# Two graph-attention layers: scores on eight array tiles, shared PSUM banks, two operations moved to GpSimd

## The reference

```
x = layernorm(x + L0(x, adj))     # q, k, v with biases; scores / sqrt(32) + beta * adj,
                                  # -9e15 where adj is 0; softmax over keys; times v
x = layernorm(x + L1(x, adj))     # q, k without bias, v with bias; scores * 384^-0.5 + adj;
                                  # rows that are all 0 give 0; softmax; times v; @ Wo.T + bo
```

## Time and profile before

| | |
|---|---|
| median of three runs | 1083.22 us (1083.09 to 1083.26) |
| the profiled execution's own time | 1081.61 us |
| its span, first to last instruction | 1079.7 us, TensorE clock granted 0.996 |
| PE, weight loads | 1051.8 us busy (97%), 914.4 (85%) |
| DVE | 935.1 (87%) |
| ACT | 445.9 (41%) |
| POOL | 533.0 (49%) |
| POOL shift (L785), scale (L791), rstd (L806) | 1664, 1474, 547 ns each, 128 times |
| DVE normalise (L657) | 486 to 526 ns, 128 times |
| DVE low part of activations (L669), first and second layer | 1607 and 550 ns |

### The profile page before, as it was taken

The page is one execution under the profiler, slowest core; times in us unless marked ns, Lnnn a source line. Parts: engine busy times, 40 slices in busy tenths (PEclk is TensorE's granted clock), DMA queues, the critical chain, the costliest instruction groups (busy, mean ns, idle before and its releaser), DMA issues.

```text
span 1079.7 us, 38267 instructions
## 1 busy us (share of the span) xinstructions
PE 1051.8 (97%) x16896; PEld 914.4 (85%) x16896; DVE 935.1 (87%) x1642; ACT 445.9 (41%) x713; POOL 533.0 (49%) x454
## 2 busy tenths in 40 slices
PE   7999999999999999999999999999999999999975
PEld 5887888888888888888888888888888888888874
DVE  4799998989899898998989899898998989878786
ACT  4454434444334443444444344443444444344321
POOL 0454554545446454454545546455454544655443
PEclk9999999999999999999999999999999999999998
DMA  7321112112021111111111121120211210010101
GB/s 243 100 70 28 55 46 66 31 51 60 17 66 39 43 61 39 44 46 43 54 43 41 44 66 39 43 61 25 58 39 43 60 44 10 17 36 2 34 31 38
DMA packets 61749, 53.32 MB, mean 49 GB/s; under 512 B 35984, under 2 KB 55440, under 8 KB 61584
## 3 DMA queue, kind: packets, MB, share of 16 engines
q1 hardware_dynamic: 60752, 49.69, 15.4%
q10 hardware_dynamic: 832, 1.18, 0.3%
HBM read 38.28 MB, written 12.58 MB: 47 GB/s over the span
## 4 chain that ended last, share of the span: by engine, by line
PE 92%; DVE 4%; issue 2%; DMA 1%; ACT 1%; POOL 1%; SPq 0%; POOLq 0%; DVEq 0%
PE ps_u L356 54%; PE ps_s L373 10%; PE ps_o L356 9%; PE ps_p L441 7%; PE ps_p L456 7%; PE ps_x L386 3%; PE ps_o L470 2%; DMA xt_in<-in_x_t 1%; DVE row_sum L693 1%; DVE probs L641 1%; POOL probs L785 1%; DVE row_max L651 1%; ACT probs L563 0%; DVE x L657 0%; DVE xt_lo L669 0%
## 5 line engine op out<-in xcount | busy, mean ns | idle before, releaser
L785 POOL TENSOR_TENSOR probs<-probs,row_max 128x768 f32<-128x768 f32 x128 | 213.0, 1664 | 298.1 <-DVE row_max L651 298.1
L791 POOL TENSOR_TENSOR probs<-probs,row_inv 128x768 f32<-128x768 f32 x128 | 188.7, 1474 | 111.1 <-DVE row_inv L701 63.5
L532 ACT COPY probs_t<-ps_p 128x768 f32<-128x768 f32 x128 | 102.7, 802 | 201.7 <-PE ps_p L441 201.7
L563 ACT ACTIVATE probs<-probs 128x768 f32<-128x768 f32 x128 | 108.5, 847 | 78.8 <-POOL probs L785 78.7
L693 DVE TENSOR_REDUCE row_sum<-probs 128x12 f32<-128x768 f32 x128 | 121.5, 949 | 22.5 <-ACT probs L563 21.6
L356 PE MATMUL ps_u<-w_hi_v,xt_lo 128*128 128x384 f32 x384 | 137.3, 358 | 1.0 <-DVE v_sb L686 1.0
L806 POOL TENSOR_TENSOR rstd<-var_eps,minus_half 128x1 f32<-128x1 f32 x128 | 70.0, 547 | 133.8 <-DVE var_eps L734 133.8
L356 PE MATMUL ps_u<-w_hi_v,xt_hi 128*128 128x384 f32 x384 | 129.1, 336 | 0.0
L356 PE MATMUL ps_u<-w_lo_v,xt_hi 128*128 128x384 f32 x384 | 128.7, 335 | 0.0
L651 DVE TENSOR_REDUCE row_max<-probs 128x12 f32<-128x768 f32 x128 | 121.3, 948 | 2.2
L356 PE MATMUL ps_u<-xt_hi,w_lo_q 128*128 128x512 f32 x285 | 121.8, 427 | 0.0
(11 more groups left out here) (78 smaller groups left out, 2034.3 us busy)
## 6 DMA issues: line engine op xcount, KB each, us to landing
x_in<-in_x SPq DMA_DIRECT2D x16, 768.0 KB, 4.6
out<-z SPq DMA_DIRECT2D x64, 192.0 KB, 1.9
xt_in<-in_x_t SPq DMA_DIRECT2D x15, 768.0 KB, 4.5
adj<-in_adj SPq DMA_DIRECT2D x64, 128.0 KB, 2.9
xt_in<-in_x_t SPq DMA_DIRECT2D x3, 256.0 KB, 4.3
q_sb<-in_wq ACTq DMA_DIRECT2D x3, 192.0 KB, 4.5
k_sb<-in_wk ACTq DMA_DIRECT2D x1, 576.0 KB, 7.1
v_sb<-in_wv SPq DMA_DIRECT2D x1, 576.0 KB, 7.0
```

Of the source, the lines that this page charges most:

```text
L532: nc.scalar.copy(probs_t[:].rearrange("p (a i) n -> p a (i n)", a=2), ps_p[:, :, 0:KT * P]).then_inc(probs_t_ready, 1)
L563: nc.scalar.activation(e, e, ACT.Exp).then_inc(exp_ready, 1)
L785: nc.gpsimd.tensor_tensor(s, s, over_keys(row_max[p]), ALU.subtract).then_inc(shifted, 1)
L791: nc.gpsimd.tensor_tensor(s, s, over_keys(row_inv[p]), ALU.mult).then_inc(probs_ready, 1)
```

## The change

- `scores`: `par` becomes `side = (hh % 2) ^ b`, and each graph of the tile writes banks of its own, so a tile's scores lie in four banks, `ps_s[:, half_of * GT + b, ...]`. `heads` reads the turned probabilities by the same `side`.
- `bias_and_max` adds the bias in two instructions, one per graph.
- PSUM is dealt out anew: `ps_s` has four banks; the turned probabilities go into its first two; heads, result and turned activations share the two banks of `ps_h` (was `ps_p`), result in bank 0, turned activations in bank 1.
- PE's order in a step: scores, first unit, result, turned activations, turned probabilities, other units, heads. The waits follow from the shared banks.
- `normalise` and the first layer's `activations_lo` go from DVE to GpSimd; `xt_lo_ready` is now two semaphores, one per layer. ACT takes the first unit out before it takes the turned activations.

```diff
-        ps_s = ps("ps_s", [P, 2, 512])
+        ps_s = ps("ps_s", [P, 4, 512])
         ps_u = ps("ps_u", [P, 2, 512])
-        ps_p = ps("ps_p", [P, GT, 512])
-        ps_x = ps("ps_x", [P, 512])
-        ps_o = ps("ps_o", [P, 512])
+        ps_h = ps("ps_h", [P, GT, 512])
...
             def scores(tile):
...
                     pe.wait_ge(biased, at(tile))
+                if at(tile) > 1:
+                    pe.wait_ge(probs_t_ready, at(tile) - 1)
...
-                            half_of, par = hh // 2, hh % 2
-                            at_key = (g * GT + b) * NODES
+                            half_of, side = hh // 2, (hh % 2) ^ b
                             last = nc.tensor.matmul(
-                                ps_s[par * NODES:(par + 1) * NODES, half_of, at_key:at_key + NODES],
+                                ps_s[side * NODES:(side + 1) * NODES, half_of * GT + b, g * NODES:(g + 1) * NODES],
...
+            def heads_read(tile):
+                pe.wait_ge(o_t_ready, at(tile) + 1)
+                if tile[0] == 1:
+                    pe.wait_ge(o_lo_ready, second_no(tile))
+
-            def turn_activations(tile):
+            def turn_activations(tile, last_heads):
...
-                pe.wait_ge(xt_lo_ready, TURN_NO[tile] - 1)
+                heads_read(last_heads)
...
-            def turn_probs(tile):
+            def turn_probs(tile, scored):
                 pe.wait_ge(probs_ready, at(tile) + 1)
-                if at(tile) > 0:
-                    pe.wait_ge(o_t_ready, at(tile))
...
+                if scored:
+                    pe.wait_ge(biased, at(scored) + 1)
...
-            def heads(tile):
+            def heads(tile, turned):
...
                 pe.wait_ge(probs_t_ready, at(tile) + 1)
+                if at(tile) > 0:
+                    pe.wait_ge(z_ready, at(tile))
+                if turned and turned[0] == 1:
+                    pe.wait_ge(xt_lo_ready[1], low_no(turned))
...
             for s in STEPS:
                 if s.cur:
                     scores(s.cur)
-                if s.turned:
-                    turn_activations(s.turned)
                 for unit in s.units[:1]:
                     make_unit(unit)
                 if s.last:
                     result(s.last)
+                if s.turned:
+                    turn_activations(s.turned, s.last)
...
# DVE
-                nc.vector.tensor_tensor(
-                    s[:].rearrange("p (a g) b k -> p a g (b k)", a=2),
...
+                for b in range(GT):
+                    done = nc.vector.tensor_tensor(
+                        s[:, :, b, :].rearrange("p (a g) k -> p a g k", a=2),
+                        ps_s[:, b::GT, 0:KT * NODES].rearrange("p a (g k) -> p a g k", g=KT),
+                        bias[:, GT * t + b, :].unsqueeze(1).unsqueeze(1).to_broadcast([P, 2, KT, NODES]), ALU.add)
+                done.then_inc(biased, 1)
...
-                if s.done:
-                    normalise(s.done)
                 for unit in s.units[:1]:
                     unit_out(unit)
+                if s.last:
+                    residual(s.last)
                 if s.turned and s.phase >= 0:
                     activations_lo(s.turned)
-                if s.last:
-                    residual(s.last)
...
# GpSimd
+                nc.gpsimd.tensor_tensor(xt_lo[p][:, :, cols], xt_in[:, :, cols], xt_hi[p][:, :, cols].bitcast(F32),
+                                        ALU.subtract).then_inc(xt_lo_ready[0], 1)
...
+                nc.gpsimd.tensor_scalar(dst, z[t % 2][:], mean_var[t % 2][:, 0:1], rstd[t % 2][:],
+                                        ALU.subtract, ALU.mult).then_inc(normed, 1)
...
             for s in STEPS:
                 if s.cur:
                     shift(s.cur)
...
+                if s.turned and s.phase >= 0:
                     add_bo(s.turned)
+                    activations_lo(s.turned)
                 if s.last:
                     inverse_deviation(s.last)
+                    normalise(s.last)
                 if s.cur:
                     scale(s.cur)
```

More of the change, by code:

```diff
@@ L89, in second_no, with low_no @@
     return TILES * tile[1] + tile[2] + 1
+def low_no(tile):
+    return TILES * (tile[1] - (tile[0] == 0)) + tile[2] + 1
 def tile_before(tile, n):
@@ L227, in two_gnn_layers_kernel @@
         max_ready = sem("max_ready")
-        xt_lo_ready = sem("xt_lo_ready")
+        xt_lo_ready = [sem(f"xt_lo_ready{l}") for l in range(2)]
         v_ready = sem("v_ready")
@@ L383, in turn_activations @@
                 pe.wait_ge(normed, at((0, c, t)) + 1)
-                pe.wait_ge(xt_lo_ready, TURN_NO[tile] - 1)
+                heads_read(last_heads)
                 for g in range(KT):
-                    last = nc.tensor.transpose(ps_x[:, g * P:(g + 1) * P], x1[c % 3][:, t, g * P:(g + 1) * P],
+                    last = nc.tensor.transpose(ps_h[:, 1, g * P:(g + 1) * P], x1[c % 3][:, t, g * P:(g + 1) * P],
                                                ident[:])
@@ L464, in result @@
                 layer = tile[0]
-                if at(tile) > 0:
-                    pe.wait_ge(z_ready, at(tile))
-                pe.wait_ge(o_t_ready, at(tile) + 1)
+                heads_read(tile)
                 if layer == 0:
                     for g in range(KT):
-                        last = nc.tensor.transpose(ps_o[:, g * P:(g + 1) * P], o_t[:, g, :], ident[:])
+                        last = nc.tensor.transpose(ps_h[:, 0, g * P:(g + 1) * P], o_t[:, g, :], ident[:])
                 else:
@@ L489, in _ @@
                     result(s.last)
+                if s.turned:
+                    turn_activations(s.turned, s.last)
                 if s.prev:
-                    turn_probs(s.prev)
+                    turn_probs(s.prev, s.cur)
                 for unit in s.units[1:]:
@@ L494, in _ @@
                 if s.prev:
-                    heads(s.prev)
+                    heads(s.prev, s.turned)
         @block.scalar
@@ L580, in _ @@
                         activations_hi((*ORDER[1], t))
+                for unit in s.units[:1]:
+                    unit_out(unit)
                 if s.turned and s.phase >= 0:
                     activations_hi(s.turned)
-                for unit in s.units[:1]:
-                    unit_out(unit)
                 if s.prev:
@@ L718, in residual @@
                 earlier = tile_before(tile, 2)
+                if earlier and earlier[0] == 0:
+                    dve.wait_ge(normed, at(earlier) + 1)
                 if earlier and earlier[0] == 1:
@@ L743, in _ @@
                 if place == (-1, 1):
-                    for t in range(TILES):
-                        activations_lo((*ORDER[1], t))
                     weights_lo("v0")
@@ L801, in add_bo, with activations_lo @@
                 nc.gpsimd.tensor_tensor(rows, rows, bo_rows[:], ALU.add).then_inc(x1_bo_ready, 1)
+            def activations_lo(tile):
+                layer, c, t = tile
+                if layer == 1:
+                    return
+                p = home((layer, c))
+                pool.wait_ge(xt_hi_ready, TURN_NO[tile])
+                pool.wait_ge(xt_loaded, 16 * c)
+                cols = slice(t * P, (t + 1) * P)
+                nc.gpsimd.tensor_tensor(xt_lo[p][:, :, cols], xt_in[:, :, cols], xt_hi[p][:, :, cols].bitcast(F32),
+                                        ALU.subtract).then_inc(xt_lo_ready[0], 1)
             def inverse_deviation(tile):
@@ L806, in inverse_deviation, with normalise @@
                 nc.gpsimd.tensor_tensor(rstd[p][:], var_eps[p][:], minus_half[:], ALU.pow).then_inc(rstd_ready, 1)
+            def normalise(tile):
+                layer, c, t = tile
+                pool.wait_ge(rstd_ready, at(tile) + 1)
+                dst = x1[c % 3][:, t, :] if layer == 0 else z[t % 2][:]
+                nc.gpsimd.tensor_scalar(dst, z[t % 2][:], mean_var[t % 2][:, 0:1], rstd[t % 2][:],
+                                        ALU.subtract, ALU.mult).then_inc(normed, 1)
             for s in STEPS:
@@ L810, in _ @@
                     shift(s.cur)
-                if s.turned:
+                if (s.phase, s.t) == (-1, 1):
+                    for t in range(TILES):
+                        activations_lo((*ORDER[1], t))
+                if s.turned and s.phase >= 0:
                     add_bo(s.turned)
+                    activations_lo(s.turned)
                 if s.last:
                     inverse_deviation(s.last)
+                    normalise(s.last)
                 if s.cur:
```

52 lines of the change are left out of this document (17 added, 35 removed).

## The result

The changed kernel took 1071.99 us (median of 5 runs, 1069.73 to 1076.03) against 1083.22 in the runs beside it: ratio 0.9898, interval 0.9887 to 0.9909. The forecast was 1084.5, 1.3 us longer than before; the kernel became 11.2 us shorter. The time lies inside the wide range (1068 to 1095), outside the forecast's own (1079 to 1090), and almost at rival B (1070.2). The profiled execution took 1069.95 us, with a span of 1068.2.

A forecast was written before the change was run, and what follows sets the result against it. PE was taken to bound the kernel (92% of the chain). Gained 19.7, lost 18.2 + 0.9 + 1.3 + 0.6 = 21.0: 1.3 us longer, 1084.5 us; own range 1079 to 1090, wide range 1068 to 1095.

The forecast's parts named there:

- rival B: Bias preparation slips in ahead of GpSimd's scaling, its first half takes 0.42, stall 0.3: 1070.2 us; chance 0.13.
- Scores on eight tiles: PE's score block shrinks from 0.86 to 0.71 us; 0.16 taken in 123 steps, 19.7 us gained.
- The new wait: PE's turned probabilities wait for DVE's bias addition in thirteen first steps of second-layer chunks: 1.40 each, 18.2 us lost.
- it waits for the scaling, and will again: DVE's bias preparation, first half: takes 1.51 us today, ending 0.28 after GpSimd's scaling, and was expected to keep waiting.
- Normalise on GpSimd: Normalise, without a row on GpSimd, was taken at 0.87 us, between 0.55 and 1.01, ahead of the scaling.
- C: Normalise on GpSimd takes 1.64 us, so the same stall grows by 0.77 x 13 = 10.0: 1094.5 us; chance 0.22.
- The boundary's 0.9: The boundary between first-layer chunks 1 and 2 adds 0.9 us lost, by the working of the new wait.
- Turned activations: On PE, moved from behind the scores to between result and probabilities: 0.02 lost per step, 64 times, 1.3 us.
- the shared `ps_h`: PE's heads wait for DVE's low part in the last second-layer step: nothing lost, bound 0.3 x 13.
- Tail: At the kernel's end the last normalise takes 0.4 more and the last steps 0.05 each: 0.6 us lost.

The follow-up runs named there:

- e5: The changed kernel without the scores of the first group of four heads from the second tile on (only its times are of use): 1044.50 us, ratio 0.9647.
- e3: The changed kernel with side = hh % 2, so scores stay in four banks but run on four array tiles: 1089.86 us, ratio 1.0063.
- e1: The changed kernel with GpSimd's scaling put ahead of its normalise in each step: 1089.88 us, ratio 1.0061.
- e2: The changed kernel with normalise back on VectorE at its old place: 1098.10 us, ratio 1.0131.
- e9: e2 plus a second, useless normalise on GpSimd between rstd and scaling, into a tile nobody reads: 1086.71 us, ratio 1.0040.
- e8: The changed kernel with second unit earlier at t=0, last second-layer low part ahead of the statistics, last two tiles normalised by DVE: 1065.03 us, ratio 0.9834.
- e7: The kernel before the change with only normalise moved to GpSimd: 1092.94 us, ratio 1.0092.
- e10: e7 with VectorE's low part put behind the residual and its statistics instead of ahead: 1080.81 us, ratio 0.9980.
- e4: The changed kernel with the first layer's low part back on VectorE, behind the residual: 1074.21 us, ratio 0.9918.

## Why the prediction was wrong

**Scores on eight tiles: right.** Last start 0.56, block 0.71, both as worked out, and e5 shows that the pace falls behind the first 32. Forecast 19.7 gained; e3 gives 17.9 by its median and 16.1 by its steps: 0.15 was measured where 0.16 was taken, and the steps that wait for the scaling or ahead of the heads gain less.

**The new wait: the step that failed** is "it waits for the scaling, and will again". It was the price of 1.51 for the first half of the bias preparation, which took 0.41 in fact, in 15 of 16 executions. What VectorE does before it came out: from the addition's start to the preparation's 6.02 us (forecast 6.17), low part 1.02 (1.0). The stall of 1.40 x 13 = 18.2 was 0.25 x 13 = 3.2, and with another releaser, the scaling. Those 15 us more than cover the miss of 12.5 (1084.5 - 1072.0); the tail, below, takes some back.

**Normalise on GpSimd was mis-sized, and that decided it.** It takes 1.66, C's price (1.64), and not 0.87; the forecast's own range ended at 1.1. C had "the same stall grows by 0.77". The sign was the other one: the forecast put preparation and scaling 0.03 us apart (its own terms give 0.06: 506.45 + 2.08 + 1.64 is 510.17, not 510.14), so 0.79 more of normalise takes the scaling out of the preparation's way (505.53 and 506.29). I had tied the preparation to the scaling as if it were a dependency, while it is a collision, and a collision is decided by which starts first. Two rivals that were costed as alternatives were one case: C's duration brings about B's order. e1, e2 and e9 show it from both sides. That the time came out near B is B's stall (0.3, measured 0.25), not B's reason: a gap of 0.03 us would have left it to chance.

The rule cited with B, in the Trainium skill's "SBUF — State Buffer", Who interferes with whom, speaks of VectorE instructions with two SBUF inputs, and is borne out in part. Behind a running scaling the second half, which has two, takes 1.84 and ends after it (58.03, above). Behind the start of a normalise it takes 1.04 and ends before it (e1: 515.50 and 515.94): slowed, not blocked. Where it starts ahead of the scaling it takes 0.75, and the scaling 1.77 instead of 1.48. The first half has one tensor input, and a running scaling holds it too (1.51), while a running `TENSOR_SCALAR` of GpSimd does not (0.41). The measurement decides.

**The boundary's 0.9 and the others.** Between first-layer chunks 1 and 2 nothing was lost (the first step of the third phase takes 8.74 instead of 10.36); the wait of 1.09 came one phase earlier, whose first step takes 10.39 instead of 9.15. Steps 0 to 11 gained 2.2 in all. Turned activations: booked as 1.3 lost; second-layer t=1 gained 0.26 instead of 0.15, t=2 and t=3 only 0.08 and 0.01. Part of t=3's loss is a step costed at nothing, the shared `ps_h` in the last second-layer step, some 0.05 and within its bound of 0.3: e5, whose score block is 0.29 shorter, gains nothing there (7.32 again), because PE waits for `xt_lo` ahead of the heads (5.4 us in 16 waits). What else t=2 and t=3 lose was not isolated. Tail: 0.6 expected, 2.3 measured, and it goes with the place of the normalise: 23.7 in e2, which has it on DVE, and 25.7 or more in every kernel that has it on GpSimd for all tiles. DVE's normalise of the last two tiles, with the other mends of e8, brings it from 26.2 to 25.1.

**Open:** why GpSimd's `TENSOR_SCALAR` of 384 columns with one tensor input takes 1.66 us where its `TENSOR_TENSOR` with two takes 1.02, and why it leaves the preparation's first half alone; the two may have one cause, which no run here isolates. In every run the first half starts 0.7 to 1.4 us after the start of such a normalise, never sooner (0.33 us after it e1's second half was slowed), so it may be the moment and not the form of the instruction that counts. Open too are PE's pause of 2.1 us and what limits the score block behind the 32nd matmul.

## What to carry over

Where two instructions on different engines slow each other only while they overlap, write down both start times and the gap between them before pricing either: a gap smaller than the uncertainty of what stands ahead (here 0.03 us against a normalise of anything from 0.55 to 1.64) makes two cases, and a longer instruction can be the better one. An operation without a row on its new engine is the first thing to bound, and each bound is to be followed through the order of starts, not only added to the sum. Before moving work onto an engine, list what its input waits for there: e7 and e10 differ by one position of a 0.55 us subtraction and by 1.1% of the time. And before a difference between two profiled executions is given to an edit, look whether it returns in every step of its kind or stands in one: the mean of e2's t=2 steps hid a single pause.

## What the runs showed of the hardware

- Small matmuls packed on eight array tiles run at the tiles' pace only for the first 32: 32 begin within 0.27 to 0.29 us, the next 16 need as long again (0.56). Going from four to eight tiles took a block of 48 from 0.86 to 0.71; 32 on eight tiles take 0.42.
- GpSimd's `TENSOR_SCALAR` with two per-partition operands takes 1.66 us for 128x384 fp32; `TENSOR_TENSOR` of that size 1.02, of twice the size 1.48. The Trainium skill's "GPSIMD Engine Reference", 4.1 Engine selection, has one-input work roughly at line rate there; 1.66 against VectorE's 0.49 for the same form says otherwise.
- A useless 1.65 us instruction on a queue made the kernel 0.9% faster (e9 against e2).
- A running GpSimd `TENSOR_TENSOR` held VectorE's `TENSOR_SCALAR` of one tensor until 0.28 us after its own end (0.41 became 1.51, 13 of 13 in e1 and in e2). A running GpSimd `TENSOR_SCALAR` left it at 0.41 (13 of 13 in the changed kernel and in e9), with starts 0.86 us into it.
- After a pause of PE of 2.1 us the granted clock was 0.50 for 3.4 us; pause and slow stretch cost 3.8 us (step 6 of e4).
